# Two-layer gated cross-attention: POOL's products of 2048 elements issued as four instructions of 512

## The chip, the cores and the metric

The kernel runs on one core of a Trainium2 chip. A core has five engines that run side by side and wait for one another by semaphores: PE (TensorE, matrix products), DVE (VectorE), ACT (ScalarE), POOL (GpSimd) and SP (SyncE, which here issues the DMAs). The metric is the device time of one execution in microseconds (us), and the median of several runs is compared. The profile comes from one profiled execution.

## The reference

The input x has 16 batches of 256 tokens with 256 features. Two layers follow one another; each adds a gated cross-attention to x and then a gated feed-forward part.

```python
x = x + tanh(g_xattn[0]) * L0_xattn(layernorm(x), ctx, ctx, mask, causal)   # 16 heads of 64
x = x + tanh(g_ffn[0])   * L0_ffn(layernorm(x))
x = x + tanh(g_xattn[1]) * L1_xattn(layernorm(x), ctx, ctx)                 # 16 heads of 16
x = x + tanh(g_ffn[1])   * L1_ffn(layernorm(x))                             # two experts and a shared one
```

The change lies in the first layer's feed-forward part. Ahead of a mixture of eight experts it mixes the 16 heads (of 16 features each) within each token:

```python
att = einsum('bthd,btgd->bthg', q, k) / 4      # 16 x 16 scores for each token
att = softmax(att)
out = einsum('bthg,btgd->bthd', att, v)
```

## The kernel before

`layer0` computes the first layer and `layer1` the second, one behind the other. Each engine has its own program, written out by hand: a `body` for one turn of a software pipeline, unrolled at both ends and run in a loop (`Fori(3, B - 1)`) in the middle. In the first layer a turn works on three batches at a time: attention of batch a, head mixing of batch b = a - 1, and experts of batch c = a - 2. A turn has `STEPS` = 20 steps `s`, and tables such as `mix_at`, `score_at` and `gather_at` say at which step an engine does which side job. Semaphores with counted values order everything between engines; each engine takes its own instructions in the order in which they are written.

The head mixing has tokens on the partitions (two tiles `t` of 128 tokens). For each tile, POOL multiplies and DVE sums:

- `query_key` (L339, the instruction at L350): all pairs of heads, 8 query heads x 16 key heads x 16 features = 2048 products a partition, written to one half `u` of the tile `prod`. There are four of these in a batch (t = 0, 1; u = 0, 1). Broadcasts over an axis of the queries and of the keys are part of the access patterns. DVE's `mix_scores` (L620) sums over the features.
- the softmax over the 16 scores (L627 to L637), with ACT's exponential (L495) in the middle.
- `weigh` (L355, the instruction at L364): 8 heads x 16 features x 16 weights = 2048 products, again four in a batch. DVE's `mix_gather` (L643) sums them into `o`, which shares its tile with `h`.

`prod` has two halves, so that POOL may fill one while DVE sums the other: the third product waits for the first sum, and the fourth for the second (`scored`, `gathered`). The semaphore `prod_ready` counts the products that are complete, eight in a batch.

In POOL's `body` a turn is: the mask of batch a, three small powers, `split_context` and a power for the next batch, the four score products and the four weighing products. In DVE's `body` the score sums lie at steps 7, 9, 11 and 12, the softmax at 12 and 13, and the gathering sums at 15, 16, 18 and 19; behind them follow `attn_final` (L722, L726) and then, at the start of the next turn, the statistics and normalisations (L552 to L592, L650, L653) ahead of the first maximum of scores (L710). PE's next turn begins with `pe.wait_ge(gathered, ...)` and the transposes of `o` (L838), followed by the query projections `q0` and `q1` and by the product with `fo` (all L137 to L139), for which DVE's L650 waits. L566 is DVE's normalisation of the next batch's x at step 7.

Of the kernel before, what the change touches and what calls it, by code (L numbers as in the profile page):

```python
# [20 lines left out]
P = 128  # L21
NT = S // P
ND = D // P
H = 16
# [3 lines left out]
HPC = P // HD0  # L28
HD = D // H
LAT = 64  # L30
E = 8
HID = 1024
NHC = HID // P
# [109 lines left out]
def layer0(nc, ins, x2):  # L143
    with ExitStack() as ctx:
# [10 lines left out]
        wq, wk, wv = pair("wq", [P, ND, INNER]), pair("wk", [P, ND, INNER]), pair("wv", [P, ND, INNER])  # L155
        fq, fdown, fup, fo = pair("fq", [P, ND, D]), pair("fdown", [P, ND, LAT]), pair("fup", [LAT, 2 * D]), pair("fo", [P, ND, D])
        wg, we = pair("wg", [P, ND, E]), pair("we", [P, ND, E * D])
        wo = sb("wo", [P, NC0, D])
        prod = sb("prod", [P, 2, H * D // 2])
        stage = prod  # L160
        bo, bq, bup, bfo, bg = sb("bo", [P, D]), sb("bq", [P, D]), sb("bup", [P, 2 * D]), sb("bfo", [P, D]), sb("bg", [P, E])
        bdown, gamma1, gamma2 = sb("bdown", [LAT, 1]), sb("gamma1", [P, ND]), sb("gamma2", [P, ND])
        gates, tg = sb("gates", [P, 4]), sb("tg", [P, 4])
# [16 lines left out]
        x1res, n, h = sb("x1res", [P, NT, D]), sb("n", [P, NT, D]), sb("h", [P, NT, D])  # L180
        statB, mvB, varB, rstdB = sb("statB", [P, NT, 6]), sb("mvB", [P, NT, 2]), sb("varB", [P, NT]), sb("rstdB", [P, NT])
        ms1, r1, ms2, r2 = sb("ms1", [P, NT]), sb("r1", [P, NT]), sb("ms2", [P, NT]), sb("r2", [P, NT])
        hT, dT = pair("hT", [P, ND, S]), pair("dT", [LAT, S])
        q, kv = sb("q", [P, NT, D]), sb("kv", [P, NT, 2 * D])
# [38 lines left out]
        prod_ready, sub_ready, aexp_done = sem("prod_ready"), sem("sub_ready"), sem("aexp_done")  # L223
# [6 lines left out]
        def piece(src, dst, rows=P):  # L230
# [5 lines left out]
                  piece(ins["fdown"], (fdown[0][:].rearrange("p c n -> p (c n)"), fdown[1][:].rearrange("p c n -> p (c n)"))),  # L236
                  piece(ins["fup"], (fup[0][:], fup[1][:]), LAT),
                  piece(ins["fo"], (fo[0][:].rearrange("p c n -> p (c n)"), fo[1][:].rearrange("p c n -> p (c n)"))),
# [10 lines left out]
        with nc.Block() as block:  # L249
# [50 lines left out]
            @block.gpsimd  # L300
            def _(pool):
                nc.gpsimd.memset(ident[:], 0.0)
                nc.gpsimd.memset(cmask[:], 0.0)
                nc.gpsimd.memset(neghalf[:], -0.5)
                pool.drain()
                nc.gpsimd.affine_select(out=ident[:], in_=ident[:], compare_op=ALU.not_equal, fill=1.0, base=0,
                                        pattern=[[-1, P]], channel_multiplier=1)
                for c in (P, S):
                    last = nc.gpsimd.affine_select(out=cmask[:, c:c + P], in_=cmask[:, c:c + P], compare_op=ALU.is_ge,
                                                   fill=-NEG, base=0, pattern=[[-1, P]], channel_multiplier=1)  # L310
                last.then_inc(consts, 1)

                def power(ready, done, src, dst, b):

                    pool.wait_ge(ready, b + 1)
                    nc.gpsimd.tensor_tensor(dst[:], src[:], neghalf[:], ALU.pow).then_inc(done, 1)

                def split_context(a):
                    if not first(a):
                        _, full, _, turn = attn.at("v3", a - 1)  # L320
                        pool.wait_ge(full, turn)
                    wait_apart(pool, pool_passed, ctx_in, 16 * (a + 1))
                    nc.gpsimd.tensor_copy(cT[0][:], ctxin[:])
                    pool.drain()
                    nc.gpsimd.tensor_sub(cT[1][:], ctxin[:], cT[0][:].bitcast(F32)).then_inc(ctx_ready, 1)

                def mask(a):

                    if not first(a):
                        score.emptied(pool, f"s{H - 2}", a - 1)  # L330
                        score.emptied(pool, f"s{H - 1}", a - 1)
                    wait_apart(pool, pool_passed, mask_in, 16 * (a + 1))
                    nc.gpsimd.tensor_scalar(mbias[:, 0:S], maskbits[:], -1.0, NEG, ALU.add, ALU.mult)
                    pool.drain()
                    nc.gpsimd.tensor_tensor(mbias[:, S:CAUSAL], cmask[:, S:CAUSAL], mbias[:, 0:P], ALU.add)
                    pool.drain()
                    nc.gpsimd.tensor_tensor(mbias[:, 0:S], cmask[:, 0:S], mbias[:, 0:S], ALU.add).then_inc(mask_ready, 1)

                def query_key(b, t, u):  # L339

                    half, piece = H // 2, NT * t + u
                    if piece < 2:
                        side.emptied(pool, "q", b)
                        side.emptied(pool, f"up{t}", b)
                    else:
                        side.emptied(pool, f"up{t}", b)
                        pool.wait_ge(scored, 4 * b + piece - 1)
                    k4 = kv[:, t, 0:D].rearrange("p (g d) -> p g d", d=HD)
                    q4 = q[:, t].rearrange("p (h d) -> p h d", d=HD)
                    nc.gpsimd.tensor_tensor(  # L350
                        prod[:, u].rearrange("p (h g d) -> p h g d", h=half, g=H),
                        q4[:, u * half:(u + 1) * half].unsqueeze(2).to_broadcast([P, half, H, HD]),
                        k4.unsqueeze(1).to_broadcast([P, half, H, HD]), ALU.mult).then_inc(prod_ready, 1)

                def weigh(b, piece):  # L355

                    t, u, half = piece // 2, piece % 2, H // 2
                    if piece < 2:
                        pool.wait_ge(att_ready, b + 1)
                    else:  # L360
                        pool.wait_ge(gathered, 4 * b + piece - 1)
                    v4 = kv[:, t, D:2 * D].rearrange("p (d g) -> p d g", d=HD)
                    a4 = att[:, t].rearrange("p (h g) -> p h g", g=H)[:, u * half:(u + 1) * half]
                    nc.gpsimd.tensor_tensor(prod[:, u].rearrange("p (h d g) -> p h d g", h=half, d=HD),  # L364
                                            a4.unsqueeze(2).to_broadcast([P, half, HD, H]), v4.unsqueeze(1).to_broadcast([P, half, HD, H]),
                                            ALU.mult).then_inc(prod_ready, 1)

                def body(a, b, c, nxt):
                    if a is not None:
                        mask(a)  # L370
                    if b is not None:
                        power(varB_ready, rstdB_ready, varB, rstdB, b)
                    if b is not None:
                        power(ms1_ready, r1_ready, ms1, r1, b)
                    if c is not None:
                        power(ms2_ready, r2_ready, ms2, r2, c)
                    if nxt is not None:
                        split_context(nxt)
                        power(varA_ready, rstdA_ready, varA, rstdA, nxt)
                    if b is not None:  # L380
                        query_key(b, 0, 0)
                        query_key(b, 0, 1)
                        query_key(b, 1, 0)
                        query_key(b, 1, 1)
                        for piece in range(4):
                            weigh(b, piece)

                split_context(0)
                power(varA_ready, rstdA_ready, varA, rstdA, 0)
                body(0, None, None, 1)  # L390
                pool.wait_ge(split_lo, NS)
                body(1, 0, None, 2)
                body(2, 1, 0, 3)
                with pool.Fori(3, B - 1) as a:
                    body(a, a - 1, a - 2, a + 1)
                body(B - 1, B - 2, B - 3, None)
                body(None, B - 1, B - 2, None)
                body(None, None, B - 1, None)

            @block.scalar  # L400
            def _(act):
# [68 lines left out]
                def before_exp(b, c, s):  # L470
# [3 lines left out]
                    if b is not None and mix_at.get(s) == "down":  # L474
                        ps, full, _, turn = side.at("down", b)
                        act.wait_ge(full, turn)
                        nc.scalar.activation(dT[0][:], ps[0:LAT, 0:S], ACT.Identity, bias=bdown[:]).then_inc(dT_hi, 1)
                    if c is not None and s == 4:
# [65 lines left out]
            def _(dve):  # L544
# [62 lines left out]
                def mix_down(b):  # L607
                    ps, _, free, _ = side.at("down", b)
                    dve.wait_ge(dT_hi, b + 1)
                    V.scalar_tensor_tensor(out=dT[1][:], in0=ps[0:LAT, 0:S], scalar=bdown[:], in1=dT[0][:].bitcast(F32),  # L610
                                           op0=ALU.add, op1=ALU.subtract).then_inc(free, 1)
# [1136 lines left out]
```

## Time and profile before

| what | value |
|---|---|
| median of 3 runs | 2658.17 us (2657.94 to 2660.88) |
| the profiled execution | 2663.2 us, span 2661.4 us |
| mean granted TensorE clock | 0.956 |
| PE busy | 2325.5 us (87%) |
| DVE busy | 1487.3 us (56%), 3906 instructions |
| ACT busy | 1268.0 us (48%) |
| POOL busy | 1019.5 us (38%), 910 instructions |
| of POOL: score products (L350) | 64, 290.3 us |
| of POOL: weighing products (L364) | 64, 287.4 us |
| DVE's sums of them (L620, L643) | 128, 292.2 us |

The span runs from the first to the last instruction. A share of busy time is a mean over both layers, of which the first takes about half, so what limits one stage is read from that stage's own rows. Rows of a timeline give a start, a duration, the instruction and, in brackets, how long its engine stood idle before it and for whom. Granted clock 1.00 is 2.4 GHz and 0.50 is 1.2 GHz.

### The profile page before, as it was taken

To read this page: it belongs to the slowest core of one execution; us is meant where nothing else is said; L and a number is where in the kernel's file an instruction comes from. 1 tells how busy PE (TensorE), PEld (TensorE's weight loads), DVE (VectorE), ACT (ScalarE), POOL (GpSimd) and SP (SyncE) were. 2 spreads that over 40 slices of the span, in tenths; PEclk is the share of its full clock that TensorE was granted. 3 is DMA by queue.
4 is the path that set the end of the run, shared out by engine and by line. 5 is a ranking of instruction groups with operands and counts; after the bars stand their busy time and mean duration, and the time that the engine had idled before them with its cause. 6 is when DMAs were issued, how large, how long until landed. Compare 5 with 4: busy or idle time off the path is not lost. (4 is left out here: it accounts for less than half of the span.)

```text
span 2661.4 us, 48220 instructions
## 1 busy us (share of the span) xinstructions
PE 2325.5 (87%) x16128; PEld 1931.7 (73%) x16128; DVE 1487.3 (56%) x3906; ACT 1268.0 (48%) x3971; POOL 1019.5 (38%) x910
## 2 busy tenths in 40 slices
PE   5888989888888898888466999999999999999998
PEld 4667777777777777776354777877777887777777
DVE  3467667666766676767635445444444544444441
ACT  5655566555556555556023444433344443334441
POOL 1355554555554455555512333222233322223320
PEclk9989999999999999999667999999999999999999
DMA  4000000000000000000040000000000000000000
GB/s 145 14 6 17 13 16 4 16 16 16 16 12 4 16 16 16 16 4 9 4 161 1 13 17 16 16 16 16 4 12 16 16 16 16 16 4 12 16 9 9
DMA packets 25856, 51.66 MB, mean 19 GB/s; under 512 B 6272, under 2 KB 7040, under 8 KB 24640
## 3 DMA queue, kind: packets, MB, share of 16 engines
q1 hardware_dynamic: 25792, 50.84, 5.7%
q8 instruction: 37, 0.61, 0.1%
q14 instruction: 27, 0.22, 0.0%
HBM read 42.44 MB, written 8.39 MB: 19 GB/s over the span
## 5 line engine op out<-in xcount | busy, mean ns | idle before, releaser
L1191 POOL TENSOR_SCALAR l_probs<-l_probs,l_rinv 128x256 f32<-128x256 f32 x512 | 238.4, 480 | 590.0 <-DVE l_rinv L1406 589.4
L1302 ACT ACTIVATE l_probs<-l_score,l_negmax 128x256 f32<-128x256 f32 x512 | 238.4, 472 | 265.0 <-DVE l_negmax L1401 265.0
L364 POOL TENSOR_TENSOR l_prod<-l_att,l_kv 128x2048 f32<-128x2048 f32 x64 | 287.4, 4527 | 180.7 <-DVE l_att L637 180.7
L350 POOL TENSOR_TENSOR l_prod<-l_q,l_kv 128x2048 f32<-128x2048 f32 x64 | 290.3, 4547 | 155.9 <-DVE l_att L620 84.1
L1606 PE MATMUL l_ffn<-l_w,l_hid 128*128 128x256 f32 x1536 | 347.9, 382 | 1.0 <-ACT l_hid L1276 1.0
L1606 PEld LDWEIGHTS l_ffn<-l_w,l_hid 128*128 128x128 f32 x1536 | 287.6, 190 | 51.0 <-issue 14.3
L1413 DVE COPY l_probsT<-l_attn 128x512 f32<-128x512 f32 x256 | 175.5, 685 | 161.1 <-PE l_attn L1569 160.9
L710 DVE CUSTOM_DVE_ANT_0 l_probs<-l_score,l_mbias 128x256 f32<-128x256 f32 (+1 forms) x512 | 161.3, 353 | 147.5 <-PE l_score L906 97.6
L1401 DVE TENSOR_REDUCE l_negmax<-l_score 128x2 f32<-128x512 f32 x256 | 175.1, 684 | 65.4 <-PE l_score L1557 65.4
L643 DVE TENSOR_REDUCE l_h<-l_prod 128x128 f32<-128x2048 f32 x64 | 146.3, 2286 | 110.7 <-POOL l_prod L364 110.7
L439 ACT ACTIVATE l_probs<-l_probs,l_negmax 128x256 f32<-128x256 f32 x256 | 130.8, 511 | 107.7 <-DVE l_negmax L710 106.5
L456 ACT COPY l_probsT<-l_attn 128x384 f32<-128x384 f32 x256 | 120.7, 471 | 112.6 <-PE l_attn L916 112.5
L137 PE MATMUL l_side<-l_we_hi,l_h2T_hi 128*128 128x256 f32 x512 | 157.5, 308 | 10.8 <-DVE l_acc L694 10.2
L1276 ACT ACTIVATE l_hid<-l_ffn,l_b 128x256 f32<-128x256 f32 x384 | 161.1, 476 | 11.9 <-PE l_ffn L139 10.0
L1569 PE MATMUL l_attn<-l_ident,l_probs 128*128 128x128 f32 x1024 | 157.8, 281 | 8.6 <-DVE l_probsT L1413 7.4
L137 PE MATMUL l_attn<-l_cT_hi,l_wk_hi 128*128 128x256 f32 x384 | 124.6, 324 | 39.0 <-DVE l_xT_lo L574 39.0
L620 DVE TENSOR_REDUCE l_att<-l_prod 128x128 f32<-128x2048 f32 x64 | 145.9, 2279 | 5.8 <-issue 3.9
L139 PE MATMUL l_side<-l_we_hi,l_h2T_lo 128*128 128x256 f32 x512 | 146.2, 286 | 0.0
L138 PE MATMUL l_side<-l_we_lo,l_h2T_hi 128*128 128x256 f32 x512 | 146.2, 286 | 0.0
L447 ACT ACTIVATE l_probs<-l_probs,l_rinv 128x256 f32<-128x256 f32 x256 | 127.6, 498 | 25.0 <-DVE l_rinv L716 25.0
L1569 PEld LDWEIGHTS l_attn<-l_ident,l_probs 128*128 128x128 f32 x1024 | 120.4, 143 | 23.5 <-issue 10.3
L1176 POOL TENSOR_TENSOR l_rstdF<-l_varF,l_neghalf 128x2 f32<-128x2 f32 x16 | 11.2, 700 | 318.3 <-DVE l_varF L1338 318.3
(271 smaller groups left out, 7527.2 us busy)
## 6 DMA issues: line engine op xcount, KB each, us to landing
l_ctxin<-in_ctx SPq DMA_DIRECT2D x32, 256.0 KB, 3.0
l_xin<-in_x SPq DMA_DIRECT2D x16, 256.0 KB, 2.7
l_x<-in_x SPq DMA_DIRECT2D x16, 256.0 KB, 2.6
x<-l_acc SPq DMA_DIRECT2D x16, 256.0 KB, 2.0
l_xin<-x SPq DMA_DIRECT2D x16, 256.0 KB, 3.3
l_x<-x SPq DMA_DIRECT2D x16, 256.0 KB, 2.6
out<-l_x SPq DMA_DIRECT2D x16, 256.0 KB, 2.0
l_hid<-in_w SPq DMA_DIRECT2D x2, 1536.0 KB, 8.6
```

The costliest lines, as they stand in the source:

```text
L137: last = nc.tensor.matmul(out, wh, xh, start=n == 0, stop=False)
L350: nc.gpsimd.tensor_tensor(prod[:, u].rearrange("p (h g d) -> p h g d", h=half, g=H), q4[:, u * half:(u + 1) * half].unsqueeze(2).to_broadc ...
L364: nc.gpsimd.tensor_tensor(prod[:, u].rearrange("p (h d g) -> p h d g", h=half, d=HD), a4.unsqueeze(2).to_broadcast([P, half, HD, H]), v4.u ...
L643: V.tensor_reduce(o[:, t, u * P:(u + 1) * P], prod[:, u].rearrange("p (x g) -> p x g", g=H), axis=AX.X, op=ALU.add).then_inc(gathered, 1)
L710: last = V.tensor_tensor_reduce(out=probs[:, j % 4, lo:hi], in0=ps[:, lo:hi], in1=mbias[:, lo:hi], scale=-HD0 ** -0.5, scalar=3e38, op0=AL ...
L1191: last = nc.gpsimd.tensor_scalar(probs[:, j % 4, t * S:(t + 1) * S], probs[:, j % 4, t * S:(t + 1) * S], rinv[:, j, t:t + 1], 1.0, ALU.mul ...
L1276: last = nc.scalar.activation(hid[:, c, :], ps[:, u * S:(u + 1) * S], ACT.Relu, bias=b1[:, c:c + 1])
L1302: last = nc.scalar.activation(probs[:, s % 4, t * S:(t + 1) * S], ps[:, t * S:(t + 1) * S], ACT.Exp, bias=negmax[:, s, t:t + 1], accum_out ...
L1401: V.tensor_reduce(negmax[:, j], ps[:].rearrange("p (t k) -> p t k", t=NT), axis=AX.X, op=ALU.max, negate=True).then_inc(max_ready, 1)
L1413: V.tensor_copy(probsT[:, j % 3, :], ps[:]).then_inc(free, 1)
L1569: last = T.transpose(ps[:, kt * S + t * P:kt * S + (t + 1) * P], probs[:, j % 4, t * S + kt * P:t * S + (kt + 1) * P], ident[:])
L1606: last = T.matmul(ps[:, 0:D], hid[:, c, t * P:(t + 1) * P], w2[:, c, :], start=c == 0, stop=c == 3 * NHC - 1)
```

## The change

Each product of 2048 elements a partition is issued as four instructions, one for every two of its eight heads (`PART = 2`, 2 x 16 x 16 = 512 elements). The waits ahead of a product stay, and the increment of `prod_ready` is on the last of the four. Nothing else is changed.

```diff
+PART = 2
@@ query_key
-                    nc.gpsimd.tensor_tensor(
-                        prod[:, u].rearrange("p (h g d) -> p h g d", h=half, g=H),
-                        q4[:, u * half:(u + 1) * half].unsqueeze(2).to_broadcast([P, half, H, HD]),
-                        k4.unsqueeze(1).to_broadcast([P, half, H, HD]), ALU.mult).then_inc(prod_ready, 1)
+                    out = prod[:, u].rearrange("p (h g d) -> p h g d", h=half, g=H)
+                    for h in range(0, half, PART):
+                        last = nc.gpsimd.tensor_tensor(
+                            out[:, h:h + PART], q4[:, u * half + h:u * half + h + PART].unsqueeze(2).to_broadcast([P, PART, H, HD]),
+                            k4.unsqueeze(1).to_broadcast([P, PART, H, HD]), ALU.mult)
+                    last.then_inc(prod_ready, 1)
@@ weigh
-                    nc.gpsimd.tensor_tensor(prod[:, u].rearrange("p (h d g) -> p h d g", h=half, d=HD),
-                                            a4.unsqueeze(2).to_broadcast([P, half, HD, H]), v4.unsqueeze(1).to_broadcast([P, half, HD, H]),
-                                            ALU.mult).then_inc(prod_ready, 1)
+                    out = prod[:, u].rearrange("p (h d g) -> p h d g", h=half, d=HD)
+                    for h in range(0, half, PART):
+                        last = nc.gpsimd.tensor_tensor(out[:, h:h + PART], a4[:, h:h + PART].unsqueeze(2).to_broadcast([P, PART, HD, H]),
+                                                       v4.unsqueeze(1).to_broadcast([P, PART, HD, H]), ALU.mult)
+                    last.then_inc(prod_ready, 1)
```

## Rows read from the trace of the kernel before

**Rows 1.** Timeline of POOL, one batch: start, us, instruction, count, idle before.

```profile
502.99 9.08 POOL L350 TENSOR_TENSOR l_prod<-l_q,l_kv 128x2048 f32<-128x2048 f32 x2 [3.91 <-DVE l_kv L616]
...
521.95 4.50 POOL L350 TENSOR_TENSOR l_prod<-l_q,l_kv 128x2048 f32<-128x2048 f32 x1 [1.26 <-DVE l_att L620]
538.65 17.99 POOL L364 TENSOR_TENSOR l_prod<-l_att,l_kv 128x2048 f32<-128x2048 f32 x4 [12.20 <-DVE l_att L637]
```

**Rows 2.** Waits, 60 to 1355 us: waiter, releaser, total us, times, longest.

```profile
POOL l_prod L364 <- DVE l_att L637: 180.7, 16, 12.3
...
DVE l_h L643 <- POOL l_prod L364: 110.7, 64, 2.7
...
PE l_side L838 <- DVE l_h L643: 33.8, 12, 16.3
```

**Rows 3.** Timeline of DVE at the end of the batch.

```profile
556.68 2.29 DVE L643 TENSOR_REDUCE l_h<-l_prod 128x128 f32<-128x2048 f32 x1 [2.16 <-POOL l_prod L364]
558.88 0.68 DVE L722 TENSOR_TENSOR l_ytmp<-l_attn,l_bo 128x512 f32<-128x512 f32 x1
...
564.10 0.69 DVE L650 TENSOR_TENSOR l_y<-l_side,l_bfo 128x512 f32<-128x512 f32 x1 [1.58 <-PE l_side L139]
...
567.12 0.42 DVE L710 CUSTOM_DVE_ANT_0 l_probs<-l_score,l_mbias 128x256 f32<-128x256 f32 x1 [0.18 <-issue]
```

**Rows 4.** Timeline of PE at the end of the batch.

```profile
550.53 7.07 PE L939 MATMUL l_attn<-l_wo,l_qT 128*128 128x256 f32 x32
559.11 0.65 PE L838 MATMUL l_side<-l_ident,l_h 128*128 128x128 f32 x4 [1.51 <-DVE l_h L643]
```

**Rows 5.** Three batches: stretch, length, busy of PE PEld DVE ACT POOL, PEclk, DMA.

```profile
494.51:572.87 78.36, 68.66 (x488) 56.90 (x488) 54.58 (x156) 45.45 (x144) 42.47 (x18) 0.98 0.04 14
...
807.90:889.34 81.44, 71.74 (x488) 59.25 (x488) 54.56 (x155) 45.42 (x144) 42.40 (x18) 0.94 0.04 13
889.34:969.20 79.86, 71.69 (x488) 59.19 (x488) 54.65 (x156) 45.54 (x144) 42.40 (x18) 0.94 0.04 13
```

**Rows 6.** POOL's groups by form, first layer: count, busy us, mean ns, idle before.

```profile
L364 POOL TENSOR_TENSOR l_prod<-l_att,l_kv 128x2048 f32<-128x2048 f32 x64 | 287.4, 4527 | 180.7 <-DVE l_att L637 180.7
...
L325 POOL TENSOR_TENSOR l_cT_lo<-l_ctxin,l_cT_hi 128x512 fp32r<-128x512 f32 x16 | 20.4, 1274 | 2.3
L337 POOL TENSOR_TENSOR l_mbias<-l_cmask,l_mbias 128x256 f32<-128x256 f32 x16 | 11.7, 732 | 2.6 <-issue 0.5
```

**Rows 7.** Timeline of POOL in the second layer, two subtractions in a row.

```profile
1785.28 1.27 POOL L1206 TENSOR_TENSOR l_x1T_hi<-l_xfT_hi,l_x0T_hi 128x512 fp32r<-128x512 f32 x1
1786.51 1.27 POOL L1206 TENSOR_TENSOR l_x1T_lo<-l_xfT_lo,l_x0T_lo 128x512 fp32r<-128x512 f32 x1
```

**Rows 8.** Timeline of DVE around the score sums of the same batch.

```profile
513.09 0.74 DVE L566 TENSOR_SCALAR l_xn<-l_xin,l_mvA,l_rstdA 128x256 f32<-128x256 f32 x2
...
532.14 2.29 DVE L620 TENSOR_REDUCE l_att<-l_prod 128x128 f32<-128x2048 f32 x1 [0.16 <-issue]
```

**Rows 9.** Timeline of DVE, the last batch's fourth score sum.

```profile
1301.80 2.29 DVE L620 TENSOR_REDUCE l_att<-l_prod 128x128 f32<-128x2048 f32 x1 [1.17 <-POOL l_prod L350]
```

**Rows 10.** Timeline of POOL, score products of the last batch.

```profile
1283.40 9.03 POOL L350 TENSOR_TENSOR l_prod<-l_q,l_kv 128x2048 f32<-128x2048 f32 x2 [7.63 <-DVE l_kv L616]
1292.70 9.07 POOL L350 TENSOR_TENSOR l_prod<-l_q,l_kv 128x2048 f32<-128x2048 f32 x2 [0.27 <-DVE l_att L620]
```

**Rows 11.** All instructions of L566: duration ns min/median/max, first and last start.

```profile
L566 DVE TENSOR_SCALAR l_xn<-l_xin,l_mvA,l_rstdA x32: 394/410/3564, 15.0 to 1144.9; 128x256 f32<-128x256 f32 x32
```

**Rows 12.** Short stretches, columns as in rows 5.

```profile
522.40:525.80 3.40, 0.91 (x11) 0.60 (x8) 2.04 (x11) 3.00 (x9) 3.40 (x1) 1.00 0.00 0
525.85:529.27 3.42, 3.42 (x19) 2.97 (x17) 2.29 (x4) 2.26 (x7) 0.60 (x1) 0.50 0.00 0
...
816.00:822.80 6.80, 6.80 (x32) 5.54 (x33) 0.66 (x3) 3.14 (x13) 6.41 (x2) 0.50 0.00 0
```

## The prediction

> **What bounds the kernel now.** The page shows no engine full over the whole span, so I read stage by stage. The change touches only the first layer (the first 1,345 us). There I first read the timeline of POOL over one batch of the middle loop [rows 1]. Per batch it holds eight products of 2048 elements: four score products that start as their inputs come, and four weighing products in one unbroken run, 538.65 to 556.64. Next the table of waits [rows 2]: each of the 64 gathering sums of DVE (L643) waited for its product, 110.7 us in all, and POOL's weighing run waits for nothing but its own start, the softmax's division. Then the timeline of DVE and of PE at the end of the batch [rows 3, 4]. The last sum runs 556.68 to 558.97. PE, done with the output projection at 557.60, stands 1.51 us until 559.11, when that sum is there, and only then computes the next batch's queries. DVE has the next batch's normalisation queued behind the same sum: L722 at 558.88, L650 at 564.10 (which itself waited 1.58 us for PE, whose work began with that sum), and the first score maximum L710 at 567.12. So the loop is one ring: division, four products on POOL, last sum, PE and DVE, scores, softmax, division. A batch lasts 78.36 us [rows 5], and the 17.99 us of the weighing run lie in it without cover.
>
> **Removed and added.** 128 instructions of 2048 elements become 512 of 512. The elements, the waits in front of a product and the number of semaphore increments stay; the increment sits on the fourth piece. What is added is what an instruction costs beyond its elements. POOL's other two-input operations give it: 732 ns for 256 elements, 1274 for 512, 4527 for 2048 [rows 6]. From 512 to 2048 that is 3253 ns for 1536 elements, 2.12 ns each, and 1274 - 512 x 2.12 = 189 ns are left for the instruction (256 elements would give 732, and do). The pattern's broadcasts therefore cost nothing now, and the pieces keep them. Successive instructions overlap a little, so I price by spacing: two subtractions of 512 without a wait between them start 1.23 us apart while each lasts 1.27 [rows 7]; the big products start (17.99 - 4.53) / 3 = 4.49 apart [rows 1, 6]. Four pieces take 4 x 1.23 = 4.92, so a product costs 0.43 us more.
>
> A POOL row's duration or its spacing makes a difference here. By durations a product would cost 4 x 1.274 - 4.527 = 0.57 us more. The Trainium skill (Perfetto Trace Analysis, GPSIMD Engine Instruction) calls the reported span of such an instruction unreliable and wants start-to-start spacing; by its way the sum over 64 weighing products is 27.7 us, by the durations 36. The rows speak for spacing too: the pair's second start lies inside the first one's duration.
>
> **The weighing run, on the path.** Sixteen pieces: 15 x 1.23 + 1.27 = 19.72 us against 17.99, so 1.73 us more per batch. The first to third sum have their own gaps (they wait for POOL and take 2.29 of 4.5 us), so nothing but the last counts, and it comes 1.73 us later. PE's 1.51 us of waiting becomes 3.24; nothing takes the delay up, since PE and DVE both begin the next batch behind that sum. All 16 batches have this run: 16 x 1.73 = 27.7 us. Bounds: no cost per piece (0), and no overlap at all (16 x 1.274 - 17.99 = 2.39 us, 38 us in all). The pair of 512 is the same operation class, size and engine, so I take its value. Less than 0 is excluded for the pieces by the line through three sizes, which has a positive rest.
>
> **The score products, covered.** The first two start at 502.99 and end at 512.07; they would end about 0.85 us later, 512.9. Their first sum comes after L566, which starts at 513.09. The fourth starts at 521.95 behind DVE's second sum, ends at 526.45 and is read at 532.14 [rows 1, 8]: 5.7 us of cover for 0.43. Cost 0; without that cover it would be 1.7 us per batch. Only the last batch, with no attention beside it, lacks cover: there the sum L620 waited 1.17 us for POOL [rows 9]. Its four products run from 1283.40 with one gap of 0.27 us [rows 10]; they grow by 4 x 0.43 = 1.72, the gap takes 0.27, and 1.45 us are paid. The mask instructions follow the run on POOL and end at about 558.6, needed by L710 at 567.12: shifted with everything, no cost. SP's queue and the DMAs are not touched.
>
> **A port held by a long instruction.** L566 lasts 410 ns at the median and 3564 once, in the first batch, while the second score product ran [rows 8, 11]. A product in four would let it through sooner, 1.9 us or more of its 3.15 us stall; it lies early in a batch where ACT and PE also wait, so I count half, -1.0.
>
> Sum of these: 27.7 + 1.45 - 1.0 = 28.1 us.
>
> **TensorE's clock.** This is the term that I can only bound. In a batch of the middle loop the granted clock stands at 1.00, except that it falls to 0.50 (1.2 instead of 2.4 GHz) for 3.4 us per batch, right after PE has been almost idle for 2.5 of 3.4 us (522.4 to 525.8, waiting for xT) [rows 12]. Most batches are alike, 78.36 us with a mean clock of 0.98. Two in succession are not: 81.44 and 79.86 us at 0.94, 3.1 and 1.5 us longer for the same work [rows 5]; in the first of them the clock was at 0.50 also from 816.0 to 822.8, at a place where the other batches run at 1.00 [rows 12]. So whether a thin place of PE's work is followed by a low stretch depends on where in time it falls, and batches that repeat every 78.36 us keep nearly the same place for many batches. With 80.1 us per batch that repetition is gone, and PE's wait in front of the next batch's queries grows to 3.24 us, longer than the one that is followed by a low stretch today. A low stretch there slows the queries that the ring waits for: up to 1.7 us. Bounds: 0 extra, and 2.5 us in each of the 13 batches in the loop and beside it (33 us). I take 1.5 us in 9 of 13, since most thin places are exposed for part of the positions: 13.5 us.
>
> **Total:** 28.1 + 13.5 = 41.6 us. The profiled execution took 2663.2 us (span 2661.4 and 1.8 around it) and would take 2704.8. The median of the runs is 2658.2, 5.0 below the profiled one; added to it the forecast is 2699.8, say 2700.
>
> **Rivals.**
> 1. Path only: the clock finds its low places as rarely as before. 2658.2 + 28.1 = 2686 (2680 to 2690). For it: apart from the two long ones the batches of the loop are alike. Against it: the new wait of 3.24 us.
> 2. The clock costs more, 2.5 us or more in nearly each batch: 2716 to 2732. The batch of 81.44 us shows the size, but it was one.
> 3. The pieces cost less than the pair shows, since they read the same tile again, 0.1 to 0.2 us per product: 2666 to 2680. No row supports it.
> 4. Free pieces: POOL overlaps the start of a piece with the one before. 2658.2 - 1.0 = 2657, no difference. It decides where the spacing of pieces is 4.49 / 4 = 1.12 us; the pair of subtractions and the chain of sizes both lie above.
> 5. Faster, the other side: the port. If a long product holds back DVE instructions, pieces of 1.2 us free them. With free pieces, L566's stall gone (-1.9) and the two long batches of [rows 5] avoided by another repetition (-4.6), the time is 2651.7. It decides only if a piece costs under 1.12 us and DVE really waits for the port. Against it: beside the products DVE ran its maxima and sums without stretching, and L566 is stretched once in 32. The Trainium skill (SBUF — State Buffer, Who interferes with whom) has the rule: a DVE instruction in a two-port mode or with two SBUF inputs and a GpSimd instruction exclude each other for the whole instruction. The stall of L566 agrees with it; the middle loop has no such pair beside a product.
> That the change doesn't do what it says is excluded by the code: eight heads in steps of two, 2 x 16 x 16 = 512 elements, and the increment on the last, on an engine that takes its instructions in order.
>
> **Chances.** Forecast (2690 to 2716) 0.50; path only 0.27; more clock 0.08; cheaper pieces 0.06; free pieces 0.05; faster 0.04. The range 2674 to 2720 holds the first two cases and half of the next two, 0.84. A measurement of this kernel can tell 0.2%, 5.3 us, from no change: faster 0.04, same 0.06 (free pieces and the edge of the cheaper ones), slower 0.90.
>
> **What would show it.** Right: 512 products at about 1.27 us starting 1.23 apart; a weighing run of 19.7; PE's wait for L643 near 3.2 us where the clock stayed up; batches of 80.1 us at a clock of 0.98 and others of 81.5 to 83 at less; the second layer unchanged. Wrong: a run near 18.0 (rival 4), batches all at 80.1 (rival 1), or DVE's L566 stretched in the middle loop, if the later end of the second score product at 512.9 reaches its start at 513.09 (a piece, 1.2 us, on DVE each batch).

## The result, and the profile after

The changed kernel takes 2705.3 us (median of 4 runs, 2702.3 to 2711.2), the kernel before, run beside it, 2658.1: the ratio is 1.018, 95% interval 1.016 to 1.020. The profiled execution of the changed kernel took 2711.2 us, the longest of its four; its span is 2709.4 us against 2661.4 before, 48.0 us more. The mean granted clock fell from 0.956 to 0.942.

From the page of the changed kernel: span, engines, and the two groups of products (count | busy us, mean ns | idle before). L353 and L369 are L350 and L364 of before; the file is 5 lines longer from there on (L571 is L566, L625 is L620, L648 is L643, L843 is L838).

```profile
span 2709.4 us, 48604 instructions
...
PE 2352.1 (87%) x16128; PEld 1952.0 (72%) x16128; DVE 1485.1 (55%) x3906; ACT 1270.2 (47%) x3971; POOL 1073.3 (40%) x1294
...
L353 POOL TENSOR_TENSOR l_prod<-l_q,l_kv 128x512 f32<-128x512 f32 x256 | 317.2, 1276 | 157.7 <-DVE l_att L625 85.3
...
L369 POOL TENSOR_TENSOR l_prod<-l_att,l_kv 128x512 f32<-128x512 f32 x256 | 314.3, 1270 | 168.3 <-DVE l_att L642 168.3
```

The pieces last 1270 and 1276 ns, as the other operations of 512 elements did [rows 6]. Where the time goes shows when the span is cut at the normalisation of the expert output (L671 before, L676 after): the start, the 13 batches of the loop, the last two batches, and the second layer. Before (start:end, length, busy time of PE, PEld, DVE, ACT, POOL, granted clock, DMA share, GB/s):

```profile
0.00:179.70 179.70, 131.32 (x831) 105.16 (x831) 87.02 (x268) 106.25 (x302) 55.07 (x43) 0.93 0.17 60
179.70:1204.10 1024.40, 904.48 (x6344) 749.25 (x6344) 709.85 (x2003) 590.71 (x1848) 550.72 (x220) 0.97 0.04 13
1204.10:1338.00 133.90, 81.69 (x521) 69.35 (x521) 86.01 (x183) 40.23 (x130) 74.81 (x20) 0.78 0.02 6
1338.00:2661.40 1323.40, 1208.00 (x8432) 1007.94 (x8432) 604.47 (x1455) 530.82 (x1695) 338.89 (x628) 0.97 0.06 20
```

And the changed kernel:

```profile
0.00:177.00 177.00, 128.15 (x831) 102.60 (x831) 85.06 (x268) 106.17 (x302) 58.65 (x67) 0.94 0.18 61
177.00:1245.40 1068.40, 933.18 (x6344) 770.75 (x6344) 709.81 (x2004) 591.81 (x1848) 594.18 (x532) 0.94 0.04 13
1245.40:1385.50 140.10, 82.59 (x521) 69.80 (x521) 85.88 (x182) 40.39 (x130) 81.44 (x68) 0.76 0.01 5
1385.50:2709.40 1323.90, 1208.20 (x8432) 1008.89 (x8432) 604.36 (x1455) 531.83 (x1695) 339.00 (x628) 0.97 0.06 20
```

The loop grew by 44.0 us, 3.4 per batch; the start became 2.7 shorter, the last two batches 6.2 longer, the second layer is all but unchanged (0.5 longer). The changes at the start are taken apart further below; not all of them come from the edit. In the loop DVE and ACT are busy for the same time as before. PE is busy for 29 us more with the same 6344 matmuls, at a clock of 0.94 instead of 0.97: the first sign that the run of products on POOL is not all of it.

The timeline of POOL in two batches of the changed kernel answers [rows 1]:

```profile
512.96 9.88 POOL L353 TENSOR_TENSOR l_prod<-l_q,l_kv 128x512 f32<-128x512 f32 x8 [3.92 <-DVE l_kv L621]
...
533.44 4.94 POOL L353 TENSOR_TENSOR l_prod<-l_q,l_kv 128x512 f32<-128x512 f32 x4 [0.85 <-DVE l_att L625]
550.13 19.65 POOL L369 TENSOR_TENSOR l_prod<-l_att,l_kv 128x512 f32<-128x512 f32 x16 [11.74 <-DVE l_att L642]
...
631.67 19.70 POOL L369 TENSOR_TENSOR l_prod<-l_att,l_kv 128x512 f32<-128x512 f32 x16 [11.74 <-DVE l_att L642]
```

The weighing run is 19.65 us against 17.99. But the two runs start 81.54 us apart, not 78.36 + 1.67 = 80.03. The rest stands in PE's clock. Stretches of the changed kernel, two pairs of neighbours in time:

```profile
510.20:513.60 3.40, 2.73 (x19) 2.15 (x18) 2.53 (x11) 2.49 (x9) 0.64 (x1) 1.00 0.00 0
513.60:517.00 3.40, 3.40 (x18) 2.67 (x18) 0.16 (x1) 2.62 (x11) 3.40 (x4) 0.50 0.00 0
...
649.70:653.10 3.40, 1.35 (x7) 0.84 (x5) 1.69 (x1) 0.00 (x0) 3.02 (x5) 1.00 0.00 0
653.50:656.90 3.40, 3.06 (x15) 3.07 (x16) 2.74 (x6) 0.59 (x1) 0.00 (x0) 0.51 0.04 10
```

The first pair lies 6 to 12 us into a batch (a batch is counted from L671, L676 after). PE runs the gate's twelve matmuls of 8 columns there (511.8 to 513.3), and the clock then stands at 0.50, 1.2 GHz, for 3.4 us. In the kernel before, seven batches in a row keep 1.00 at that place, and three of the thirteen do not. The second pair is the wait for the last gathering sum: the clock falls just as PE takes up the transposes of `o` and the next batch's queries. The wait itself, on PE's timeline, first with and then without low clock in the output projection ahead of it:

```profile
563.29 7.82 PE L944 MATMUL l_attn<-l_wo,l_qT 128*128 128x256 f32 x32
572.24 0.65 PE L843 MATMUL l_side<-l_ident,l_h 128*128 128x128 f32 x4 [1.14 <-DVE l_h L648]
...
653.84 1.11 PE L843 MATMUL l_side<-l_ident,l_h 128*128 128x128 f32 x4 [2.79 <-DVE l_h L648]
```

A low stretch during the output projection only fills PE's wait (7.82 us instead of 7.07 in [rows 4], then 1.14 of waiting). It costs nothing. Two batches of the changed kernel, one without and one with the low clock behind the last sum (compare [rows 5]):

```profile
504.50:586.00 81.50, 71.81 (x488) 59.12 (x488) 54.54 (x155) 45.53 (x144) 45.73 (x42) 0.94 0.04 13
586.00:669.00 83.00, 71.56 (x488) 59.50 (x488) 54.66 (x156) 45.59 (x144) 45.88 (x42) 0.94 0.04 14
```

All 13 batches of the loop have the early low stretch, which starts 8.2 to 9.5 us in. Five of them have a further one behind the wait for the last sum and are 82.6 to 84.6 us long; the other eight last 81.35 to 81.70. In four of these eight the early stretch lasts 6.8 us instead of 3.4, and the one behind the wait for xT (the transposed x, DVE's L574) is missing; they last no longer than the rest.

### The profile page after: what moved, and what is told of

Same layout as the page of the kernel before. It is cut to its first block and busy times, and to the rows that moved or that the text cites. A ratio compares the mean times of both kernels' runs of the same rounds, so it can differ in the third digit from the quotient of the medians.

```text
span 2709.4 us, 48604 instructions
## 1 busy us (share of the span) xinstructions
PE 2352.1 (87%) x16128; PEld 1952.0 (72%) x16128; DVE 1485.1 (55%) x3906; ACT 1270.2 (47%) x3971; POOL 1073.3 (40%) x1294
## 5 line engine op out<-in xcount | busy, mean ns | idle before, releaser
L369 POOL TENSOR_TENSOR l_prod<-l_att,l_kv 128x512 f32<-128x512 f32 x256 | 314.3, 1270 | 168.3 <-DVE l_att L642 168.3
L353 POOL TENSOR_TENSOR l_prod<-l_q,l_kv 128x512 f32<-128x512 f32 x256 | 317.2, 1276 | 157.7 <-DVE l_att L625 85.3
L648 DVE TENSOR_REDUCE l_h<-l_prod 128x128 f32<-128x2048 f32 x64 | 146.3, 2286 | 137.6 <-POOL l_prod L369 137.6
L625 DVE TENSOR_REDUCE l_att<-l_prod 128x128 f32<-128x2048 f32 x64 | 145.9, 2280 | 8.2 <-issue 3.9
L452 ACT ACTIVATE l_probs<-l_probs,l_rinv 128x256 f32<-128x256 f32 x256 | 127.5, 498 | 31.2 <-DVE l_rinv L721 31.2
```

The source lines that it names most:

```text
L353: last = nc.gpsimd.tensor_tensor(out[:, h:h + PART], q4[:, u * half + h:u * half + h + PART].unsqueeze(2).to_broadcast([P, PART, H, HD]), ...
L369: last = nc.gpsimd.tensor_tensor(out[:, h:h + PART], a4[:, h:h + PART].unsqueeze(2).to_broadcast([P, PART, HD, H]), v4.unsqueeze(1).to_bro ...
```

## The experiments

Theory: the run of four weighing products is longer by 1.67 us (0.42 per product), and the ring pays that in full in each batch; the rest is TensorE's clock, which falls at thin places of PE's work in more batches than before. Rival A: the pieces cost more than their own time on some other engine (a port, the semaphores). Rival B: the clock has nothing to do with it, and the ring has a second wait that grows with the run.

**Half of the change each.** e1 changes only the weighing products, e2 only the score products:

```diff
-                    nc.gpsimd.tensor_tensor(prod[:, u].rearrange("p (h d g) -> p h d g", h=half, d=HD), ...).then_inc(prod_ready, 1)
+                    for h in range(0, half, PART):        # e1: L364 alone, PART = 2; e2: the same at L350 alone
+                        last = nc.gpsimd.tensor_tensor(out[:, h:h + PART], ...)
+                    last.then_inc(prod_ready, 1)
```

> Only the weighing products are issued in four pieces, the score products whole. Theory (the weighing run is on the ring and 16 pieces make it 1.7 us longer; the longer batch then meets the low clock more often): nearly all of the change's 47 us are here, 2698 to 2708 us, batches of 81.5 us. Rival (issuing pieces beside DVE costs time wherever it is done): half of the 47 us, about 2682.

> Only the score products are issued in four pieces. Theory (they are covered by 5 us and more): 1.4 us in the last batch and a shorter stall of L566 in the first, so 2654 to 2664 us and batches of 78.4. Rival (pieces cost time wherever they are): about 2682.

Measured: e1 2705.8 us, ratio 1.017 (1.016 to 1.019), the whole of the change. e2 2659.1 us, 1.000 (0.999 to 1.001), with 16 x 4 products in pieces and, over the whole kernel, nothing to pay for them. One batch of e1 and one of e2:

```profile
509.50:591.00 81.50, 71.71 (x488) 59.09 (x488) 54.51 (x155) 45.51 (x144) 44.03 (x30) 0.94 0.04 13
```

```profile
729.80:808.20 78.40, 68.67 (x488) 56.94 (x488) 54.60 (x156) 45.51 (x144) 44.23 (x30) 0.98 0.04 14
```

So the cost hangs on the weighing run alone; that of the score products is covered, as [rows 8] said. Rival A would have had to show in e2 too.

**The same delay with whole products.** e3 leaves the products whole and puts four multiplications of 128 elements ahead of the weighing run. They are added work: they overwrite the tile q, which nobody reads any more at that point.

```diff
+                        if piece == 0:
+                            unused, same = q[:].rearrange("p t n -> p (t n)"), kv[:, 0]
+                            for k in range(4):
+                                part = slice(k * 128, (k + 1) * 128)
+                                nc.gpsimd.tensor_tensor(unused[:, part], same[:, part], same[:, part], ALU.mult)
```

> The kernel before with all products whole, and four multiplications of 128 elements on POOL ahead of the weighing run, whose result nobody reads: 4 x 0.42 = 1.7 us per batch, as much as the pieces add. Theory (only the length of the ring and the clock behind it count, not the pieces): the same time as the changed kernel, 2698 to 2712 us, batches of 81.5 us and a mean clock near 0.94. Rival 1 (the length alone, the clock's loss in the changed kernel has another cause): 2658 + 27 = 2685, batches of 80.1. Rival 2 (pieces disturb DVE): also 2685.

Measured: 2690.7 us, 1.012 (1.010 to 1.013), less than expected. Timeline of POOL, then two batches one after the other:

```profile
549.07 1.47 POOL L364 TENSOR_TENSOR l_q<-l_kv 128x128 f32<-128x128 f32 x4 [12.17 <-DVE l_att L642]
550.50 17.93 POOL L369 TENSOR_TENSOR l_prod<-l_att,l_kv 128x2048 f32<-128x2048 f32 x4
```

```profile
503.40:584.60 81.20, 71.59 (x488) 59.36 (x488) 54.62 (x155) 45.41 (x144) 43.79 (x22) 0.94 0.04 13
584.60:664.40 79.80, 70.10 (x488) 57.89 (x488) 54.70 (x156) 45.50 (x145) 43.92 (x22) 0.96 0.04 14
```

The delay is 1.43 us (from 549.07 to 550.50), a little short of the change's 1.67. The batches without the early low stretch last 79.77 us, 1.42 more than 78.35: the ring pays the delay once, with no second wait, against rival B. Eight of the 13 have the early low stretch and last about 81.25, 1.5 us more. So a delay of whole products brings the clock's cost with it, but in eight batches, not in 13, and the wait for the last sum is never followed by a low stretch.

**Other sizes of piece.** e4 issues two pieces of 1024 (PART = 4), e10 eight of 256 (PART = 1), both in all eight products.

> Each product in two instructions of 1024 elements instead of four of 512. By the line through the sizes a piece of 1024 is spaced 2.32 us, a product costs 4.64 instead of 4.49, the run 0.58 us more, 16 x 0.58 = 9 us. Theory with the clock: batches of 78.9 us leave the favourable position sooner than those of 78.36, so some more batches meet an extra low stretch: 2670 to 2685. Path only: 2668.

Measured: 2701.8 us, 1.016 (1.014 to 1.017), far more than expected. The run and one batch:

```profile
553.47 18.57 POOL L369 TENSOR_TENSOR l_prod<-l_att,l_kv 128x1024 f32<-128x1024 f32 x8 [12.01 <-DVE l_att L642]
```

```profile
507.80:589.80 82.00, 71.67 (x488) 59.58 (x488) 54.62 (x156) 45.52 (x144) 43.65 (x26) 0.94 0.04 12
...
571.60:575.00 3.40, 1.45 (x10) 1.00 (x8) 2.88 (x2) 0.00 (x0) 2.03 (x4) 1.00 0.00 0
575.40:578.80 3.40, 3.40 (x19) 3.40 (x18) 2.28 (x7) 0.98 (x2) 0.70 (x1) 0.50 0.03 8
```

The run grew by 0.58 us, as the pieces' spacing says (2.31 us for 1024 elements). The batch grew by 3.6 us. Three places of low clock lie in all of its first 12 loop batches at nearly the same distance from the start, within 0.5 us: 9.5 us (behind the gate), 33.4 (behind the wait for xT, as before) and 67.6 (behind the wait for the last sum; the last two rows). A third of the change's extra run brings nine tenths of its loss (43 of 47 us). That is the clearest sign that the time follows the places of the low clock and not the run's length alone; the expectation (2670 to 2685) counted them as rare for so small a shift.

**The clock at the gate taken away.** In e5 and e6 the gate's twelve matmuls of step 5 stream 256 columns instead of 8; wg is stored behind we, the logits are the last 8 columns of the product, and the others are not read. e5 is the kernel before with this, e6 the changed one.

```diff
-        wg, we = pair("wg", [P, ND, E]), pair("we", [P, ND, E * D])
+        we = pair("we", [P, ND, E * D + E])
...
-                    V.tensor_tensor(glog[:], ps[:, 0:NT * E].rearrange("p (t e) -> p t e", t=NT), ...)
+                    V.tensor_tensor(glog[:], ps[:].rearrange("p (t n) -> p t n", t=NT)[:, :, D - E:D], ...)
...
-                            moe_product("gate", c, wg, E)
+                            moe_product("gate", c, [w[:, :, E * D + E - D:E * D + E] for w in we], D)
```

> The kernel before, and the 12 gate matmuls at step 5, which stream 8 columns each, stream 256 (248 columns of an expert next to them in memory; the 8 logits are read from the last columns), so that PE is not thin there. Theory (the low stretch some 8 to 12 us into a batch comes from this thin place): it disappears, also in the two or three long batches; 2648 to 2660 us, no batch above 79 in the loop. Rival (the low stretch comes from elsewhere, or the wider matmuls cost what they stream): long batches remain, or 12 x 0.1 us per batch more, 2658 to 2680.

> The changed kernel with the same wide gate matmuls. Theory (1.7 us per batch by the longer weighing run, 1.5 by the low stretch early in the batch, and in some batches 1.4 by one at the wait for the last gathering sum): batches fall from 81.6 to 80.1, some stay at 81.5; 2683 to 2694 us. Rival (the extra time of the changed kernel is not the clock's): 2700 to 2708, unchanged.

Measured: e5 2652.4 us, 0.997 (0.996 to 0.998); e6 2669.1 us, 1.004 (1.003 to 1.006), 36 us less than the changed kernel and below what was expected. PE's timeline at the gate, before and e5:

```profile
502.17 0.25 PE L137 MATMUL l_side<-l_wg_hi,l_h2T_hi 128*128 128x8 f32 x1
502.28 0.25 PE L138 MATMUL l_side<-l_wg_lo,l_h2T_hi 128*128 128x8 f32 x1
```

```profile
499.72 0.28 PE L137 MATMUL l_side<-l_we_hi,l_h2T_hi 128*128 128x256 f32 x1
499.84 0.29 PE L138 MATMUL l_side<-l_we_lo,l_h2T_hi 128*128 128x256 f32 x1
```

The matmuls start 0.12 us apart instead of 0.11, so the twelve wider ones cost about 0.1 us together. No batch of e5 or e6 has the early low stretch. e5 loses the three long batches of before (79.65, 81.44 and 79.86 us), 5.9 us together, pays about 0.1 us in each of the 13, and its loop is 4.8 us shorter in the profiles. In e6, nine of 13 batches also keep the clock at 1.00 behind the wait for xT, which was not filled; two batches in a row, the first without and the second with that stretch and one behind the last sum:

```profile
414.00:492.60 78.60, 68.86 (x488) 56.91 (x488) 54.44 (x155) 45.24 (x144) 45.78 (x42) 0.98 0.04 14
492.60:574.30 81.70, 70.35 (x488) 58.65 (x488) 54.61 (x155) 45.33 (x144) 45.84 (x42) 0.96 0.04 14
```

The expectation had left the xT stretch in each batch. That it is gone in nine makes up about 13 of the 36 us (9 x 1.5), so e6 less the changed kernel is not the price of the gate's stretch alone; e5 against before is the cleaner pair.

**Both thin places filled.** e7 (from the kernel before), e8 (from the changed one) and e9 (from the two pieces of e4) have the wide gate and in addition, at step 11, sixteen matmuls of 256 columns while PE waits for xT. Their result isn't read.

```diff
+                def keep_busy(use, c):
+                    ps, _, free, turn = side.at(use, c)
+                    pe.wait_ge(free, turn)
+                    for _ in range(16):
+                        T.matmul(ps[:, 0:D], h2T[0][:, 0, 0:P], we[0][:, 0, 0:D], start=True, stop=True)
...
+                        if c is not None and nxt is not None and s == 11:
+                            keep_busy("we4", c)
```

> The kernel before with the wide gate and 16 further matmuls of 256 columns on PE at step 11, where it waits 2.5 us for xT; nobody reads their result. Theory (each batch of the kernel before pays 1.5 us for the low stretch that follows this wait): it disappears, batches of 76.9 us, 2630 to 2642 us, faster than the kernel before. Rival (that low stretch is hidden): 2650 to 2660.

> The changed kernel with the same two additions. Theory: what is left between this and the same additions on the kernel before is the length of the weighing run, 16 x 1.7 = 27 us and 1.5 in the last batch, plus up to 1.4 us in batches where the longer wait for the last gathering sum is followed by a low stretch: 2658 to 2675 us, batches of 78.6. Rival (the pieces cost something else as well): over 2680.

> Two instructions of 1024 for each product, with the wide gate and the 16 further matmuls at step 11. Two pieces alone gave 2701.8 us, 43 more than before, where their weighing run is only 0.6 us longer. Theory (the rest was low stretches that repeated at the same places in every batch, which these additions take away): batches of 76.95 + 0.6 = 77.5 us and 2630.7 + 16 x 0.6 = 2640 us (2636 to 2650). Rival (two pieces cost time in another way): 2665 or more.

Measured: e7 2630.7 us, 0.989 (0.987 to 0.991), **faster than both kernels**; e8 2657.2 us, 1.000 (0.999 to 1.001); e9 2655.2 us, 0.999 (0.998 to 1.000). PE's timeline in e7 around the fill:

```profile
513.40 2.15 PE L895 MATMUL l_side<-l_we_hi,l_h2T_hi 128*128 128x256 f32 x16
515.95 0.39 PE L137 MATMUL l_attn<-l_cT_hi,l_wk_hi 128*128 128x256 f32 x1 [0.41 <-DVE l_xT_lo L577]
```

The 2.5 us wait for xT is 0.41 us now, and no low stretch follows it. The loops of e7 and e8 (13 batches each):

```profile
177.20:1177.40 1000.20, 909.07 (x6552) 756.84 (x6552) 709.41 (x2003) 589.14 (x1848) 551.93 (x220) 0.99 0.04 14
```

```profile
178.60:1200.60 1022.00, 924.08 (x6552) 766.73 (x6552) 709.14 (x2004) 589.10 (x1848) 595.29 (x532) 0.97 0.04 13
```

A batch of e7 is 76.95 us, one of e8 78.65, within 0.3 us for all of them. In neither does the low clock hit a place that counts; what is left of it in their loops lies in the last value and the output projection, ahead of PE's wait for the last sum. The difference of the loops is 21.8 us, 1.68 per batch: in the loop the price of the change without the clock is the run's length and nothing else. Over the whole kernel it is 26.5 us.

e9 was expected to be faster than it was (2636 to 2650). Between single batches of 77.55 us (76.95 and the 0.58 of its run) lie mostly two longer ones; eight of 13 have a low stretch behind the wait for the last sum and last 79.05. A batch of each sort:

```profile
494.30:571.80 77.50, 71.00 (x504) 58.96 (x504) 54.50 (x155) 45.30 (x144) 43.62 (x26) 0.98 0.04 14
571.80:650.90 79.10, 70.91 (x504) 59.33 (x504) 54.58 (x156) 45.41 (x144) 43.66 (x26) 0.98 0.04 14
```

The wait for the last sum (1.95 us in the longer one) was not filled in these kernels, and in these batches it is hit, while in those of e7 and e8 it is not. So e9 stands 24.5 us above e7, where the longer runs alone are 9: the two fills don't free an edit from the clock's price.

**Eight pieces.**

> Each product in eight instructions of 256 elements, nothing else changed. By the line through the sizes a piece of 256 is spaced 0.69 us, a product costs 5.5 us instead of 4.49 and the weighing run is 4.1 us longer, 16 x 4.1 = 66 us, and 3 in the last batch. Theory with the clock: batches of 78.36 + 4.1 = 82.5, or 84 with the low stretch early in the batch: 2730 to 2755 us. Length alone: 2727.

Measured: 2757.8 us, 1.037 (1.035 to 1.039), just above the range. The run and one batch:

```profile
568.28 21.91 POOL L369 TENSOR_TENSOR l_prod<-l_att,l_kv 128x256 f32<-128x256 f32 x32 [11.16 <-DVE l_att L642]
```

```profile
522.60:607.90 85.30, 73.23 (x488) 60.60 (x488) 54.56 (x155) 45.59 (x144) 50.31 (x74) 0.92 0.04 13
```

The run grew by 3.92 us, the batch by 6.95: 3.0 us of low clock (the early stretch and the one behind the last sum). The runs by number of pieces are 17.99, 18.57, 19.67 and 21.91 us for one, two, four and eight, so 1, 3 and 7 added pieces per product cost 0.58, 1.68 and 3.92 us in four products: 0.14 to 0.15 us per added instruction each time (sizes 1024, 512 and 256).

## Why the prediction held, and where it was off

It gave 2700 us in 2674 to 2720; 2705.3 were measured. On the profiled executions it had 41.6 us more, and 48.0 were found. The run and its place on the ring were predicted rightly. The clock's share was not: its size for one stretch was right, the count and the place were wrong, and part of the miss is hidden by a start that was shorter for another reason.

- **Cost of a piece, by spacing.** Predicted 1.23 us apart, a run of 19.72; measured 1.23 apart ((19.65 - 1.27) / 15), and 19.64 to 19.70 in the loop. 16 runs at 1.67 are 26.7 us; 27.7 had been said. The Trainium skill (Perfetto Trace Analysis, GPSIMD Engine Instruction) wants start-to-start spacing instead of the reported durations; this case agrees: the durations would have made the weighing runs 36 us longer, and e8 stands 26.5 above e7 for the whole change.
- **The ring takes it whole.** Shown by e3 (79.77 against 78.35 for a delay of 1.43) and by e8 against e7 (1.68 per batch).
- **Score products covered.** Shown by e2. Its other half, the last batch without cover, had 1.45 us: in the changed kernel two of that batch's sums wait for POOL, 1.82 and 1.80 us, where one waited 1.17 [rows 9], and from the first product's start to the fourth sum's it takes 19.75 us instead of 18.40, 1.35 more. Of the 6.2 us of the last two batches, 3.3 are their two weighing runs and 1.35 this; some 1.5 are left, which I put down to the clock (0.76 instead of 0.78 there) without a run that shows it.
- **The stall of L566.** Predicted -1.0; it was worth 1.8. Its two instructions in the first batch, beside the second score product, before and after, on DVE's timeline:

```profile
121.15 3.89 DVE L566 TENSOR_SCALAR l_xn<-l_xin,l_mvA,l_rstdA 128x256 f32<-128x256 f32 x2
```

```profile
119.39 2.07 DVE L571 TENSOR_SCALAR l_xn<-l_xin,l_mvA,l_rstdA 128x256 f32<-128x256 f32 x2
```

  The pair takes 1.8 us less, and the first score sum follows right behind it. e2, with the score products alone in pieces, has 2.08; e1 and e3, with them whole, have 3.92 and 3.88. Counting half for what ACT and PE do meanwhile was too little.
- **A shorter start that isn't the change's.** The changed kernel is ahead by 1.8 us already at the first batch's expert input, before the first score product starts on POOL (115.58 before, 113.83 after), so before the edit has done anything:

```profile
102.72 0.62 DVE L598 TENSOR_SCALAR l_h<-l_n,l_r 128x256 f32<-128x256 f32 x2
```

```profile
100.95 0.62 DVE L603 TENSOR_SCALAR l_h<-l_n,l_r 128x256 f32<-128x256 f32 x2
```

  In the profiles of e1, e2 and e3 the same instruction starts at 101.68, 102.48 and 100.80, with no order by the edit. It is a difference between single executions, and the forecast could not have it.
- **The clock: the term that was mis-sized.** Predicted 1.5 us in 9 of 13 batches, 13.5. In the loop it is 22.2. Counted is what comes on top of the one stretch behind xT that a usual batch of the kernel before pays as well: 13 batches of 78.35 would have taken 1018.6 us before, and 13 of 80.03 would take 1040.4 now (78.35 + 1.68, the 1.68 from e8 and e7); the loops took 1024.4 and 1068.4, so this share of the clock went from 5.8 to 28.0. The size for one stretch was right (1.5 us at the gate in e3, 1.5 behind xT by e5's 78.47 and e7's 76.95, 1.4 to 1.5 behind the last sum), the count was not. I had argued that with longer batches the repetition is gone and the thin places are exposed in part of the positions. It was not gone: the gate's place is hit in all 13 batches, five more are paid behind the last sum, and no batch of 80.1 us exists, which I had named as a sign of being right. In the first batch another clock gave back some 0.8 us: the kernel before has a low stretch of 6.8 us at 129.9, as e1 has at 129.0; the changed kernel and e2 have none there, and between L574 at 134.4 and a maximum of scores (L710) at 138.6, both by before's times, both gain 0.75. The stretch from 100 to 140 us, before and after:

```profile
100.00:140.00 40.00, 32.73 (x230) 25.42 (x228) 27.04 (x90) 29.72 (x97) 21.79 (x9) 0.91 0.07 21
```

```profile
100.00:140.00 40.00, 31.52 (x233) 24.05 (x232) 28.26 (x94) 31.54 (x102) 23.12 (x20) 1.00 0.07 21
```

- **Sum on the profiled executions:** 26.7 (runs) + 1.4 (last batch) - 1.8 (stall) + 22.9 (clock: 22.2 - 0.8 + 1.5) - 1.8 (start) + 0.5 (second layer) = 47.9 of 48.0. The clock's 22.2 and 1.5 are what the other terms leave of their stretches, so the closing of the sum is no test of them; for the loop e7 and e8 are. Against the 41.6 of the forecast the clock has 9.4 more, the runs 1.0 and the stall 0.8 less, and the start takes off 1.8. That 2700 lies within 6 us of the result is in part luck.
- **Where the clock falls.** I had placed the danger at PE's wait for the last sum, which was to be 3.24 us. It was 2.79 where the clock had stood at 1.00 (PE is later at its projection by the 0.42 us that it waits longer for ACT's kT ahead of it, 1.65 instead of 1.23) and 1.14 where the output projection itself had run slowly. It is followed by a low stretch in five batches. The place that costs in each batch is the gate, which I had not named, though it is where the two long batches of before had lost 1.5 us each and more [rows 12]; a third one, the first of the loop (79.65 us), I had missed. I had read from those rows that places move, and not which place it was.
- **Rivals.** Path only (2686) falls by the trace. Free pieces and faster fall with the run's length.

What stays open: which batch length brings a low stretch behind a thin place. 78.35 us escape at the gate seven times on end, 81.95 and 85.3 are hit each time, and no rule here tells that ahead. The traces give one hint. In the kernel before, the stretch behind xT starts a little later in each batch, 31.2, 31.3, 31.5, 31.6 and 31.8 us in, and the next batch is the one of 81.44 us with the stretch at the gate. In e2 it reaches 31.9 twice, and each time the next batch is such a one (81.45 and 81.22 us). So the places drift against the batch, and which one is hit depends on the batches before. Why they do was not looked into. Filling the wait for the last sum was not tried.

## What to carry to other kernels

Splitting an instruction on an engine that the loop waits for costs a fixed amount per added instruction (0.15 us on POOL here), and the loop pays the sum of them in each turn; price it by the spacing of such instructions. Then look at where PE's clock already falls in single turns of the loop: those places are candidates in every turn once the turn's length changes, even by 0.6 us, and the loss can be larger than the edit's own. Giving PE something to stream at such a place (wider operands for thin matmuls, spare matmuls in a wait) made this kernel 1.1% faster than before. On top of it the split into four cost only its run's length (e8), but the split into two still met the clock at the place that was left unfilled (e9).

## What the runs showed of the hardware

**Low clock behind a place where PE is mostly busy.** The gate's twelve matmuls stand in the profile at 0.25 us each and 0.11 us apart, and in the changed kernel PE is busy for 2.73 of the 3.40 us at their place; a stretch at 1.2 GHz follows in all 13 batches. With 256 columns each they start 0.12 us apart, and none follows. The same place in e5, and the stretch behind it:

```profile
497.70:501.10 3.40, 2.75 (x18) 2.26 (x18) 2.44 (x10) 2.47 (x9) 0.66 (x1) 1.00 0.00 0
501.10:504.50 3.40, 3.40 (x31) 2.80 (x30) 0.23 (x2) 3.09 (x12) 3.40 (x1) 1.00 0.00 0
```

PE's busy time, 2.73 and 2.75 us, doesn't tell the two apart. The narrow matmuls are not always followed by a low stretch: in the kernel before it is three batches of 13.

**A DVE instruction held by POOL until the product in progress ends.** The longest of the 32 instances of L566 lies in the first batch, beside the second score product. By the size of the score pieces it took 3564 ns at 2048 elements [rows 11], 2423 at 1024, 1348 at 512 and 817 at 256, and it ends 0.15 us behind the POOL instruction that was running (before: 124.71 and 124.56). The median is about 410. All instances of that instruction with pieces of 512, of 1024 and of 256 (duration ns min/median/max, first and last start):

```profile
L571 DVE TENSOR_SCALAR l_xn<-l_xin,l_mvA,l_rstdA x32: 395/414/1348, 14.3 to 1186.0; 128x256 f32<-128x256 f32 x32
```

```profile
L571 DVE TENSOR_SCALAR l_xn<-l_xin,l_mvA,l_rstdA x32: 394/411/2423, 14.1 to 1184.0; 128x256 f32<-128x256 f32 x32
```

```profile
L571 DVE TENSOR_SCALAR l_xn<-l_xin,l_mvA,l_rstdA x32: 398/410/817, 14.0 to 1225.7; 128x256 f32<-128x256 f32 x32
```

It falls with the piece, staying under one piece's time (4.53, 2.31 by spacing, 1.27 and 0.73 us) plus its own 0.41. But with pieces the other instruction of the pair is held as well, by the piece before: 1579 ns at 1024, 802 at 512 and 812 at 256, where it took 401 behind the whole product. The pair takes 3.89, 3.92, 2.07 and 1.55 us, so two pieces gained nothing. The Trainium skill (SBUF — State Buffer, Who interferes with whom) says that a DVE instruction in a two-port mode and a GpSimd instruction exclude each other for a whole instruction, and counts `tensor_scalar` among those that can enter such a mode; these rows agree with the exclusion. In this kernel four pieces were worth 1.8 us once, against 26.5 paid.
